# Gated cross attention with routed experts on one Trainium2 core: the maximum is subtracted in place by VectorE instead of by products on PE

## What is computed

```python
def xattn(q, k, v):        # q: normalised x; k, v: the context
    qh, kh, vh = proj(q, Wq, bq), proj(k, Wk, bk), proj(v, Wv, bv)
    scores = jnp.abs(jnp.einsum('bhsd,bhtd->bhst', qh, kh) / math.sqrt(D_K))
    attn = jax.nn.softmax(scores, axis=-1)
    out = jnp.einsum('bhst,bhtd->bhsd', attn, vh)
    return concat(out) @ Wo.T + bo
def ffn(x):                # 8 experts, the best 2 by softmax(x @ w_router)
    h = jax.nn.gelu(jnp.einsum('te,ieh->tih', xf, w1) + b1)
    out = jnp.einsum('tih,ihe->tie', h, w2) + b2
    return jnp.sum(out * weights[..., None], axis=1)
x = x + tanh(g_xattn) * xattn(layernorm(x), ctx, ctx)
x = x + tanh(g_ffn) * ffn(layernorm(x))
```

## Time and profile before

| | us |
|---|---|
| median of 3 runs (lowest, highest) | 790.35 (789.66, 791.15) |
| the profiled execution's own time | 792.86 |
| its span, first to last instruction | 791.1 |
| PE busy in the span | 708.2 (90%) |
| DVE busy | 478.0 (60%) |
| ACT busy | 334.8 (42%) |
| POOL busy | 311.9 (39%) |
| mean granted PE clock | 0.937 of full speed |

### The profile page before, as it was taken

One profiled execution on the slowest core, in us unless ns is written; L12 is line 12 of the kernel. 1 busy time (PEld: TensorE's weight loads), 2 busy tenths in 40 slices (PEclk: granted clock), 3 DMA queues, 4 the chain that ended last, 5 costly groups with the idle time before them and its releaser, 6 DMA issues.

```text
span 791.1 us, 21359 instructions
## 1 busy us (share of the span) xinstructions
PE 708.2 (90%) x6686; PEld 635.4 (80%) x6687; DVE 478.0 (60%) x1231; ACT 334.8 (42%) x696; POOL 311.9 (39%) x423
## 2 busy tenths in 40 slices
PE   4469999999999997349999999999999999999993
PEld 3358888888888887338899998999998999989982
DVE  6257777777676664535555665556655566655561
ACT  2137767767675653123333333333333333333330
POOL 6322465656655555601323333223332233322333
PEclk8669999999998987569999999999999999999997
DMA  3242453445443342262233232232322333323322
GB/s 104 38 149 77 144 165 123 136 136 172 151 135 109 116 129 68 96 202 42 49 52 54 40 54 47 48 54 40 54 47 47 54 46 48 49 47 53 55 30 27
DMA packets 57398, 65.02 MB, mean 82 GB/s; under 512 B 8853, under 2 KB 53054, under 8 KB 57217
## 3 DMA queue, kind: packets, MB, share of 16 engines
q1 hardware_dynamic: 42585, 45.08, 19.1%
q0 software_dynamic: 14656, 19.21, 14.8%
q10 hardware_dynamic: 104, 0.04, 0.0%
HBM read 38.34 MB, written 25.54 MB: 81 GB/s over the span
## 4 chain that ended last, share of the span: by engine, by line
PE 54%; issue 1%; DVE 1%; DMA 1%; POOL 1%; ACT 0%; POOLq 0%; SPq 0%; DVEq 0%; ACTq 0%
PE banks L1275 26%; PE banks L1299 25%; PE banks L1287 2%; POOL routed L616 1%; DMA out_dram<-y,meta 0%; DMA x_row<-routed 0%; DVE h_lo L1236 0%; DMA routed<-row,pos 0%; POOL out_dram L1188 0%; PE banks L1092 0%; DVE h_hi L1234 0%; DVE x_lo L1241 0%; PE banks L1023 0%; POOLq L526 0%; ACT hid L1212 0%
## 5 line engine op out<-in xcount | busy, mean ns | idle before, releaser
L1212 ACT ACTIVATE hid<-banks,bias_t 128x256 f32<-128x256 f32 x312 | 131.0, 471 | 268.4 <-PE banks L1275 268.3
L1188 POOL DMA_INDIRECT out_dram<-y,meta x78 | 123.2, 1580 | 219.1 <-DVE y L1256 204.2
L1275 PE MATMUL banks<-x_hi,w_hi 128*128 128x256 f16 x624 | 171.6, 275 | 4.2 <-DVE x_lo L1241 4.2
L1275 PE MATMUL banks<-x_lo,w_hi 128*128 128x256 f16 x624 | 171.6, 275 | 0.0
L1275 PE MATMUL banks<-x_hi,w_lo 128*128 128x256 f16 x624 | 171.5, 275 | 0.0
L1299 PE MATMUL banks<-w_lo,h_hi 128*128 x624 | 170.1, 273 | 0.0
L1299 PE MATMUL banks<-w_hi,h_hi 128*128 x624 | 170.1, 273 | 0.0
L1299 PE MATMUL banks<-w_hi,h_lo 128*128 x624 | 170.1, 273 | 0.0
L1236 DVE TENSOR_TENSOR h_lo<-hid,h_hi 128x512 f16<-128x512 f32 x156 | 108.1, 693 | 5.4
L1252 DVE SCALAR_TENSOR_TENSOR y<-banks,b_b 128x256 f32<-128x256 f32 x78 | 32.8, 421 | 124.5 <-PE banks L1299 124.5
L1234 DVE CAST h_hi<-hid 128x512 f16<-128x512 f32 x156 | 66.9, 429 | 33.0 <-ACT hid L1212 30.3
(11 more groups left out here) (188 smaller groups left out, 1085.0 us busy)
## 6 DMA issues: line engine op xcount, KB each, us to landing
stage<-in_L_ffn_w_dram SPq DMA_DIRECT2D x32, 512.0 KB, 4.5
x_row<-routed SPq DMA_DIRECT2D x39, 265.0 KB, 2.8
x_in<-in_x_dram SPq DMA_DIRECT2D x16, 256.0 KB, 3.2
x_res<-in_x_dram SPq DMA_DIRECT2D x16, 256.0 KB, 3.4
out_dram<-x_res SPq DMA_DIRECT2D x16, 256.0 KB, 2.5
routed<-pad_rows SPq DMA_DIRECT2D x9, 265.0 KB, 4.1
out_dram<-y,meta POOLq DMA_INDIRECT x78, 3.8
routed<-row,pos POOLq DMA_INDIRECT x64
```

Source lines behind the costliest of these rows:

```text
L1188: pool.indirect_dma_start(out[:, :], bass.IndirectOffsetOnAxis(ap=meta[:, pj, b, E:E + 1].bitcast(U32), axis=0), y[:, pj, b], None, comput ...
L1212: ins = act.activation(hid[:, c], S[:, q, c % PER * SLOTS:(c % PER + 1) * SLOTS], ACT.Gelu_apprx_tanh, bias=k.bias_t[:, bass.ds(e * HC + c ...
L1275: mm = pe.matmul(S[:, q, c % PER * SLOTS:(c % PER + 1) * SLOTS], w[:, bass.ds(e, 1), i, c * P:(c + 1) * P].rearrange("p a n -> p (a n)"), ...
```

## The change

After the maximum DVE subtracts it from the absolute scores in place, one `tensor_tensor` over 128 x 16 x 77 with the maximum broadcast over the keys (`shift_scores`). The two `split_top`, `turn_top`, `copy_top` and the ten products per tile with `spread_top` are gone, and with them the semaphores between them and the setup of `ident_bf`, `top_t` and `spread_top` on POOL, two small DMAs among it. `turn_probs` now waits for `shift_sb` and consists of ten turns.

```diff
@@ setup_phase, POOL
-                pool.tensor_copy(k.ident_bf[:], k.ident[:]).then_inc(made, 1)
-                pool.memset(k.top[:], 0.0).then_inc(made, 1)
-                pool.memset(k.top_t[:], 0.0).then_inc(made, 1)
...
-                pool.memset(k.spread_top[:], 0.0).then_inc(top_made, 1)
...
-                for part in range(1, 3):
-                    pool.dma_start(k.spread_top[part * HEADS:(part + 1) * HEADS], k.spread_top[0:HEADS])\
-                        .then_inc(top_copied, 16)
@@ attention_phase, ACT: even(j) and odd(j)
-                    if token_tile(i - 1):
-                        copy_top(i - 1)
@@ DVE
                 def top_scores(i):
                     ready(dve, prob_abs, i)
-                    ready(dve, top_ps, i - 2)
-                    dve.tensor_reduce(top_part(i, 0), prob[:, i % 2, 0:SCORES].rearrange("p (h k) -> p h k", k=KEYS),
-                                      AX.X, ALU.max).then_inc(top_sb, 1)
-
-                def split_top(i, a):
-                    ready(dve, top_sb, i, 3, a)
-                    dve.tensor_tensor(top_part(i, a), top_part(i, a - 1), top_halves[:, i % 2, a - 1, :, 1],
-                                      ALU.subtract).then_inc(top_sb, 1)
+                    dve.tensor_reduce(top[:, i % 2], heads_of(i), AX.X, ALU.max).then_inc(top_sb, 1)
+
+                def shift_scores(i):
+                    ready(dve, top_sb, i)
+                    dve.tensor_tensor(heads_of(i), heads_of(i), top[:, i % 2].unsqueeze(2).to_broadcast([P, HEADS, KEYS]),
+                                      ALU.subtract).then_inc(shift_sb, 1)
@@ DVE even(j)
                     if here:
-                        split_top(i, 1)
+                        shift_scores(i)
                     if routed_pair:
                         route(j - 4, 9, 8)
-                    if here:
-                        split_top(i, 2)
@@ PE: turn_top(i) and its calls go; turn_probs(i)
                         if g == 0:
-                            ready(pe, prob_abs, i)
+                            ready(pe, shift_sb, i)
                         for c in range(n):
-                            pe.matmul(T[:, g, c * P:(c + 1) * P], prob[:, i % 2, (first + c) * P:(first + c + 1) * P],
-                                      k.ident[:], is_transpose=True, start=(c == 0), stop=False, skip_group_check=True)
-                        if g == 0:
-                            ready(pe, top_t_sb, i)
-                        for c in range(n):
-                            mm = pe.matmul(T[:, g, c * P:(c + 1) * P], k.spread_top[:, (first + c) * P:(first + c + 1) * P],
-                                           top_t[:], start=False, stop=(c == n - 1), skip_group_check=True)
+                            mm = pe.transpose(T[:, g, c * P:(c + 1) * P],
+                                              prob[:, i % 2, (first + c) * P:(first + c + 1) * P], k.ident[:])
                         mm.then_inc(pt_ps, 1)
```

More of the change, by code:

```diff
@@ L298, in _ @@
                     .then_inc(k.factors1, 1)
-                pool.memset(k.spread_top[:], 0.0).then_inc(top_made, 1)
-                pool.wait_ge(top_made, 1)
-                pool.memset(k.spread_top[0:HEADS], -1.0).then_inc(top_made, 1)
-                pool.wait_ge(top_made, 2)
-                pool.affine_select(out=k.spread_top[0:HEADS], in_=k.spread_top[0:HEADS], compare_op=ALU.is_ge, fill=0.0,
-                                   base=0, pattern=[[1, PCH * P]], channel_multiplier=-KEYS).then_inc(top_made, 1)
-                pool.wait_ge(top_made, 3)
-                pool.affine_select(out=k.spread_top[0:HEADS], in_=k.spread_top[0:HEADS], compare_op=ALU.is_ge, fill=0.0,
-                                   base=KEYS - 1, pattern=[[-1, PCH * P]], channel_multiplier=KEYS).then_inc(top_made, 1)
-                pool.wait_ge(top_made, 4)
-                for part in range(1, 3):
-                    pool.dma_start(k.spread_top[part * HEADS:(part + 1) * HEADS], k.spread_top[0:HEADS])\
-                        .then_inc(top_copied, 16)
                 pool.wait_ge(consts, 2)
@@ L314, in _ @@
                 place_values(pool, k, value_pieces()[0:POOL_PIECES], k.v_placed[1])
-                pool.wait_ge(top_copied, 32)
             @block.vector
@@ L443, in attention_phase @@
     PROJ, TURN, NORM, ROUTE = (S[:, i] for i in range(4))
-    MAX_T = T[:, 2, PAIR:PAIR + P // 2].bitcast(BF16)
     n_bias = E * HC
@@ L460, in attention_phase @@
         stats, mv, var_eps, rstd, neg_mean = k.stats, k.mv, k.var_eps, k.rstd, k.neg_mean
-        top, top_t = k.top, k.top_t
+        top = sb("top", [P, 2, HEADS])
         x_res = sb("x_res", [P, 2, 2, D])
@@ L505, in attention_phase @@
             k.stats1, k.factors1, k.norm1, k.xt_ps, k.xt_sb, k.q_ps, k.q_sb, k.q_lo_sb)
-        score_ps, top_ps, x2t_ps, pt_ps, av_ps, logit_ps, ot_ps, wo_ps, rank_ps = (
-            sem(n) for n in ("score_ps", "top_ps", "x2t_ps", "pt_ps", "av_ps", "logit_ps", "ot_ps", "wo_ps", "rank_ps"))
-        top_t_sb, x2t_sb, pt_sb, prob_abs, ot_sb, router_exp, w_hi, norm2 = (
-            sem(n) for n in ("top_t_sb", "x2t_sb", "pt_sb", "prob_abs", "ot_sb", "router_exp", "w_hi", "norm2"))
-        top_sb, den_sb, attn_sb, x2_sb, stats2, router, places = (
-            sem(n) for n in ("top_sb", "den_sb", "attn_sb", "x2_sb", "stats2", "router", "places"))
+        score_ps, x2t_ps, pt_ps, av_ps, logit_ps, ot_ps, wo_ps, rank_ps = (
+            sem(n) for n in ("score_ps", "x2t_ps", "pt_ps", "av_ps", "logit_ps", "ot_ps", "wo_ps", "rank_ps"))
+        x2t_sb, pt_sb, prob_abs, ot_sb, router_exp, w_hi, norm2 = (
+            sem(n) for n in ("x2t_sb", "pt_sb", "prob_abs", "ot_sb", "router_exp", "w_hi", "norm2"))
+        top_sb, shift_sb, den_sb, attn_sb, x2_sb, stats2, router, places = (
+            sem(n) for n in ("top_sb", "shift_sb", "den_sb", "attn_sb", "x2_sb", "stats2", "router", "places"))
         factors2, res_bo, row_sb, w_lo = (sem(n) for n in ("factors2", "res_bo", "row_sb", "w_lo"))
@@ L712, in _, with heads_of @@
             def _(dve):
-                top_halves = top[:].rearrange("p i n -> p (i n)").bitcast(BF16).rearrange(
-                    "p (i a h b) -> p i a h b", i=2, h=HEADS, b=2)
-                def top_part(i, a):
-                    return top[:, i % 2, a * HEADS:(a + 1) * HEADS]
+                def heads_of(i):
+                    return prob[:, i % 2, 0:SCORES].rearrange("p (h k) -> p h k", k=KEYS)
                 def top_scores(i):
                     ready(dve, prob_abs, i)
-                    ready(dve, top_ps, i - 2)
-                    dve.tensor_reduce(top_part(i, 0), prob[:, i % 2, 0:SCORES].rearrange("p (h k) -> p h k", k=KEYS),
-                                      AX.X, ALU.max).then_inc(top_sb, 1)
-                def split_top(i, a):
-                    ready(dve, top_sb, i, 3, a)
-                    dve.tensor_tensor(top_part(i, a), top_part(i, a - 1), top_halves[:, i % 2, a - 1, :, 1],
-                                      ALU.subtract).then_inc(top_sb, 1)
+                    dve.tensor_reduce(top[:, i % 2], heads_of(i), AX.X, ALU.max).then_inc(top_sb, 1)
[3 more added lines that the diff above has]
+                                      ALU.subtract).then_inc(shift_sb, 1)
                 values = V[:, 0:HEADS * VW].rearrange("p (h w) -> p h w", w=VW)
```

22 lines of the change are left out of this document (removed).

## The result

The changed kernel takes 803.77 us (median of 6, 797.73 to 814.8) beside 791.66 for the kernel before on the same chip (median of 6): ratio **1.0127**, 95% interval 1.0096 to 1.0158. It is slower, by more than the range allowed. Measured again on another chip it took 801.36 (median of 9) against 794.57: 1.0071 (1.0036 to 1.0106). So about 1%, with a wider spread than the kernel before has. That spread has a companion in the records: the mean granted clock of the first six executions was 0.897, 0.911, 0.913, 0.914, 0.916 and 0.918, and their times 814.8, 809.85, 804.94, 802.59, 800.15 and 797.73 in the same order.

The account below looks back on a forecast made before the run. PE sets odd halves, VectorE 0.6 us ahead; a chain through VectorE ends even halves. Pairs +3.2, first pairs -1.2, tail -2.2, clock -3.8 and +5.1 sum to +1.1 on 790.35: 791.4 us, range 785 to 799.

Parts of the forecast that it names:

- Subtraction 1.44 us: On VectorE, one added subtraction of 128x1232 per tile takes 1.44 us, with ends 1.26 and 1.75.
- Rival 4: The subtraction takes 1.75 us by contention with GpSimd, 0.3 more in each of 12 odd halves: 795 us, chance 0.06.
- Odd half 8.03 to 8.69, set by VectorE, PE idle 1.3: Second tile's scores to next pair's first: VectorE's later logits copy adds 0.66 us, PE idle 1.3 ahead of even scores.
- Rival 3: PE remains the bound and the subtraction is hidden: the full 20 us gained, 770 us, chance 0.04.
- Even half -0.39, the subtraction hidden ahead of `q_hi`: Without the turn of the maxima, values follow scores 0.39 us sooner; the subtraction fits VectorE's wait and costs nothing.
- An odd half with a fall now pays 0.33: Where the clock falls, VectorE is already 1.27 later, so 0.33 of 1.6 us is paid; three such halves: -3.8.
- First pairs -1.2, tail -2.2: Before pair 4, less spreading but six subtractions, -1.2 us; in the last pair PE leads again, -2.2 us.
- three more even falls at 1.6, +4.8: PE's gaps grow to 1.3 us, clock falls 4 in 12 at each edge; three more in even halves, +4.8 us.
- Rival 1: The clock falls in most even halves, 1.6 us each, eight falls instead of four: 798 us, chance 0.25.
- worst part: The part of Rival 1 that the prediction left out of its range of 785 to 799 us.
- the exchange on the two engines is near zero: PE's saving against VectorE's subtraction: an undisturbed full pair takes 0.27 us more, +3.2 over twelve pairs.

Follow-up runs that it names:

- addshift: The kernel before plus VectorE's in-place subtraction, with the turn of the maxima and all spreading products kept: 798.88 us, ratio 1.0051.
- nospread: The kernel before without its spreading products, VectorE's work kept and no subtraction added: 801.21 us, ratio 1.0081 to the kernel before.
- fill10b: The changed kernel plus ten products of ones per tile, ahead of the turns of the probabilities: 795.90 us, ratio 1.0017 to the kernel before.
- changed_low_late: The changed kernel with place ahead of q_lo and the weights' low half behind the logits' copy: 776.24 us, ratio 0.9841 to the kernel before.
- changed_place_fill: The changed kernel with place ahead of q_lo and ten products of ones per tile: 788.34 us, ratio 0.9976 to the kernel before.
- changed_place_early: The changed kernel with one VectorE operation, place, moved ahead of q_lo: 796.38 us, ratio 1.0029 to the kernel before.
- place_early: The kernel before with one VectorE operation, place, moved ahead of q_lo: 784.38 us, ratio 0.9891 to the kernel before.
- its filled form: changed_low_late plus ten products of ones per tile at the turn of the probabilities: 773.27 us, ratio 0.9796 to the kernel before.

## Why the prediction was wrong

By its own steps:

- **Subtraction 1.44 us**: right (median 1442 ns; a single one of 2.48 us raises the mean over 60 to 310 us to 1474). Rival 4, 1.75, is out; its 0.3 for GpSimd's transfers was my guess, and no run shows it on VectorE.
- **Odd half 8.03 to 8.69, set by VectorE, PE idle 1.3**: right, 8.70 with a gap of 1.19. Rival 3 is out.
- **Even half -0.39, the subtraction hidden ahead of `q_hi`**: right, 7.75, values at 0.51. Of VectorE's wait for `q_hi` 0.65 is left; "some 2 us" less 1.44 is 0.6. The gain had two reasons where one was named: `addshift` gets 0.34 of it with the turn still there.
- **An odd half with a fall now pays 0.33**: nearly; 9.06 to 9.18 against 8.69 is 0.37 to 0.49, in five of eleven where four were forecast. The 9.05 of pair 12 is no fall.
- **First pairs -1.2, tail -2.2**: neither came so. In this execution the part up to pair 4 came out at -6.2, half of it ahead of the first maximum, where the setup that went had been put at 0, and the tail at +0.9. Over all profiles the two stand at about -3 and +2 (means of nine against five, given above), so the tail goes the other way. The changed kernel's share in this was not tried by itself.
- **The clock, "at 1.3 I take 4 in 12 at each", three more even falls at 1.6, +4.8**: this is the step that failed, in number and in price. Six of twelve even halves were disturbed, and a fall there lasts one stretch of 3.4 us (+1.7) or two (+2.7). Against the forecast of -0.39 x 12 = -4.7 the even halves came to +6.1, so the falls took 10.8 us in this execution, where 4.8 had been taken. This execution missed the forecast of +1.1 by 4.9: 6.0 in the even halves, 0.8 in the odd ones and 3.1 in the tail, less 5.0 ahead of pair 4. In the execution at 814.8 three even halves took 11.59, 3.85 above the undisturbed, with three stretches at 0.50 each. I took 4 in 12 at a gap of 1.3, hardly more than the 3 in 12 at 0.75, and took the price from halves in which one stretch fell. `nospread` shows how far that was off: with a single gap of 1.3, and none at the other edge, eight of twelve even halves were disturbed. The other executions of the first six weren't profiled; that their times rise as their clocks fall is what ties the rest of the 803.77 to the same step.

Rival 1 named the cause, and its condition, "from the third additional fall on". Its 798 is within the 797.73 to 814.8 measured but below the median, for the price again. The "worst part" that the range leaves out of it was my estimate, and no run shows a figure for it; the highest execution, 814.8, is 15.8 above the range. Of its two reasons, the longer gap and the full products removed from ahead of it, `nospread` and `fill10b` bear out both together, and `changed_low_late` (no products, gap 0.28, 7 us at 0.50) speaks for the gap. That the exchange on the two engines is near zero was right: undisturbed pairs take 0.2 to 0.3 more, where 0.27 was forecast. That `fill10b` stands at 1.0017, next to the forecast's 1.1 / 792.86, 1.0014, is luck: it carries ten products that the forecast kernel hasn't, and seven odd halves that pay 0.96. What stays open: why a fall lasts one stretch in one half and two in the next, and why the filler's place moves the falls from one half to the other.

## What to carry to other kernels

In this kernel, taking products off PE lengthened a gap that another engine ends, from 0.75 to 1.3 us in each pair, and cost more at the clock than it gained in the undisturbed halves (an estimated 11 us against 4 in `nospread`). So look first at which gaps of PE the change makes longer, look up the granted clock behind them, price a fall by the half it hits (1.7 to 2.7 us in these even halves), and test with the products left out alone. The undisturbed halves were forecast to about 0.05 us from one execution, and the time was still missed by over 1%. And when work moves to an engine that sets the next wait, look for what stands in that engine's path without need: here one operation of 1.21 us moved back, with `place` moved ahead, turned a loss of 0.7 to 1.3% into a gain of 1.6%.

## What the runs showed of the hardware that I had not expected

- Less work on PE made the kernel slower (`nospread`, 1.0081), and work for nothing made it faster (`fill10b` against the changed kernel, 1.0071 to 1.0017; `changed_place_fill` against `changed_place_early`, 1.0029 to 0.9976).
- GpSimd's scattered row transfers take longer beside the subtraction, 1.32 us where they took 1.03. Groups by line, 60 to 310 us: the kernel before, the changed one, then `addshift` (the kernel before with the subtraction) and `onehead` (the changed one nearly without it):

```profile
L616 POOL DMA_INDIRECT routed<-row,pos x52 | 53.5, 1029 | 22.7 <-issue 11.9 <-DVE seen L814 10.8
```

```profile
L597 POOL DMA_INDIRECT routed<-row,pos x48 | 63.3, 1320 | 20.9 <-issue 11.0 <-DVE seen L781 10.0
```

```profile
L617 POOL DMA_INDIRECT routed<-row,pos x48 | 64.3, 1339 | 20.9 <-issue 11.0 <-DVE seen L822 10.0
```

```profile
L597 POOL DMA_INDIRECT routed<-row,pos x52 | 54.8, 1054 | 22.7 <-issue 11.9 <-DVE seen L782 10.8
```

What rival 4 feared for VectorE isn't seen there (median 1442 ns). It is GpSimd's transfers that take longer, off the path, and this comes and goes with the subtraction: 1339 ns with it alone, 1054 nearly without. The order matters as well: `place_early`, without the subtraction, has 1133, and `changed_low_late` and its filled form, with it, 1133 and 1060.
